# Second layer: row transfers held to their steps, norms of the finished batch moved into the expert stretch

## The reference, cut to what matters

```python
scores = jnp.einsum('bhqd,bhkd->bhqk', q, k) / sqrt(HD)
attn = jax.nn.softmax(scores, axis=-1)
ao = jnp.einsum('bhqk,bhkd->bhqd', attn, v)
x1 = _layernorm(x + ao @ Wo + bo, g1, be1)
...
topk_p, topk_i = jax.lax.top_k(gate_probs, K)          # K = 2 of E = 8
h = jax.nn.gelu(jnp.einsum('bsd,edf->bsef', x1, W1) + b1, approximate=False)
y = jnp.einsum('bsef,efd->bsed', h, W2) + b2
moe_out = jnp.einsum('bse,bsed->bsd', comb, y)
return _layernorm(x1 + moe_out, g2, be2)
...
x = x + _layernorm(_L0_ffn_ref(_layernorm(x, axis=-1), ...), axis=-1)
```

## Time and profile before

| what | value |
|---|---|
| median of 3 runs | 2871.48 us (2869.06 to 2873.38) |
| the profiled execution's own time | 2869.59 us |
| its span | 2867.9 us |
| busy: DVE, ACT, PE | 2243.4 us (78%), 1236.5 us (43%), 1195.6 us (42%) |
| POOL busy | 289.9 us (10%) |
| L1309, the maxima | 512 of 1219 ns |
| L1196, the exponentials | 512 of 1027 ns |

### The profile page before, as it was taken

How to read it: one execution, slowest core, us unless ns; L and a number is a source line. 1 busy time by engine, 2 the same in 40 slices (tenths; PEclk the granted TensorE clock), 3 DMA queues, 4 the chain that set the end, 5 groups by cost and what they waited for, 6 DMA issues and landing times. The chain is left out here.

```text
span 2867.9 us, 37860 instructions
## 1 busy us (share of the span) xinstructions
PE 1195.6 (42%) x7272; PEld 536.4 (19%) x7272; DVE 2243.4 (78%) x15187; ACT 1236.5 (43%) x3176; POOL 289.9 (10%) x425
## 2 busy tenths in 40 slices
PE   3010100101010000101004887788876887778697
PEld 1000000000000000000001111223421342133365
DVE  5999999999999999999975899856657665864133
ACT  1333333333333333333360556656655664567542
POOL 0000000000000000000010020031023212201211
PEclk9999999999999999999996899979987998889898
DMA  5000000000000000000034020103110212001100
GB/s 135 1 1 1 1 1 1 1 1 1 1 1 1 1 1 1 1 1 1 1 68 103 1 67 20 24 22 89 26 44 23 74 37 52 18 17 30 33 1 23
DMA packets 79603, 66.11 MB, mean 23 GB/s; under 512 B 8126, under 2 KB 64232, under 8 KB 79368
## 3 DMA queue, kind: packets, MB, share of 16 engines
q1 hardware_dynamic: 76296, 57.40, 8.3%
q0 software_dynamic: 3072, 6.30, 0.7%
HBM read 34.77 MB, written 28.57 MB: 22 GB/s over the span
## 5 line engine op out<-in xcount | busy, mean ns | idle before, releaser
L1309 DVE TENSOR_REDUCE nm_half<-pair 128x2 f32<-128x1024 f32 x512 | 611.7, 1219 | 224.1 <-PE pair L1557 188.6
L203 ACT ACTIVATE ex<-row,nmax 128x65 f32<-128x65 f32 x960 | 336.0, 350 | 923.8 <-DVE nmax L305 837.3
L1196 ACT ACTIVATE pt<-pair 128x1024 f32<-128x1024 f32 x512 | 510.2, 1027 | 389.2 <-PE pair L1567 357.9
L263 DVE SCALAR_TENSOR_TENSOR junk<-ex,tab 128x65 f32<-128x65 f32 x2850 | 620.0, 218 | 1.4 <-issue 0.4
L366 PE MATMUL p_s<-tab,bdg 128*128 128x32 f32 x120 | 31.9, 406 | 829.2 <-DVE tab L268 829.2
L1533 PE MATMUL p_o<-pt,va 128*9 128x512 f32 x2048 | 299.2, 659 | 9.7 <-ACT pt L1196 8.3
L268 DVE TENSOR_TENSOR tab<-raw,rz 128x1 f32<-128x1 f32 (+1 forms) x1890 | 284.8, 151 | 3.2 <-issue 1.1
L297 DVE SCALAR_TENSOR_TENSOR junk<-ex,rz,row 128x65 f32<-128x65 f32 x930 | 265.4, 285 | 3.0 <-issue 2.7
L1557 PE MATMUL pair<-ks,qs 48*128 48x512 bf16 x1024 | 212.8, 420 | 123.3 <-ACT pt L1196 75.4
L1567 PE MATMUL pair<-qs,ks 50*128 50x512 bf16 x1024 | 209.7, 414 | 62.4 <-DVE nm_half L1309 30.4
L263 DVE DVE_READ_ACCUMULATOR junk<-ex,tab 128x1 f32 x2850 | 233.8, 82 | 0.3
(11 more groups left out here) (254 smaller groups left out, 1908.1 us busy)
## 6 DMA issues: line engine op xcount, KB each, us to landing
parts_dram<-parts SPq DMA_DIRECT2D x48, 256.0 KB, 3.6
qs<-parts_dram SPq DMA_DIRECT2D x32, 192.0 KB, 4.8
ks<-parts_dram SPq DMA_DIRECT2D x32, 192.0 KB, 5.4
hid<-xs_dram SPq DMA_DIRECT2D x15, 256.0 KB, 2.9
ys_dram<-hid SPq DMA_DIRECT2D x15, 256.0 KB, 2.4
h_dram<-f SPq DMA_DIRECT2D x20, 128.0 KB, 2.5
x<-in_x SPq DMA_DIRECT2D x4, 512.0 KB, 8.4
w_W<-in_W SPq DMA_DIRECT2D x1, 2048.0 KB
```

Of the source, the lines that this page charges most:

```text
L203: nc.scalar.activation(ex[:, r % 2, :], row[:, r % 2, 1:], ACT.Exp, bias=nmax[:, r % 2:r % 2 + 1], accum_out=z[:, r % 2:r % 2 + 1]).then_i ...
L263: nc.vector.scalar_tensor_tensor(junk[:, g, :], ex[:, k, :], 1.0, tab[:, g, r:r + ROW], ALU.mult, ALU.mult, accum_out=raw[:, g:g + 1]).the ...
L1196: nc.scalar.activation(pt[:, kt % 2, :, tokens(t)], pair[fill.pair][:, :, :], ACT.Exp, scale=SCALE).then_inc(s_exp, 1)
L1309: nc.vector.reduce_max(nm_half[:, t, hp % 2, :, q], pair[fill.pair][:, :, :], AX.X, negate=True)\
```

## The change

It does four things. A step `SC` or `YG` carries a number, the count of exponentials that precede its step, and POOL waits for `s_exp` to reach it before it issues the step's two DMAs. The scatters are spread over steps 14 to 21 of the tables. The norms k=1 and k=2 of the finished batch move from steps 14 to 23 of `TAIL` to steps 27 to 47, and the two `ADD` move by a step. The phases start later and closer (29 to 54, every 5 steps), and the decays of `busy` and the floor of the maxima are changed. Between slots and the first scatter POOL also increments its pace semaphore once more.

```diff
--- before.py
+++ after.py
@@ -598,17 +598,18 @@
 
 AFTER = {0: [("AT", 0), ("AT", 1)], 1: [("WO", 0)], 2: [("LNS", 0, 0), ("WO", 1), ("LNS", 0, 1)],
          4: [("LND", 0)], 5: [("LNN", 0, 0)], 6: [("LNN", 0, 1), ("XT", 0)], 7: [("XT", 1), ("GL", 0), ("GL", 1)],
-         9: [("GA",), ("GE",)], 10: [("GB",)], 11: [("GC",)], 13: [("RK",)], 14: [("RT",)],
-         15: [("SC", 0), ("SC", 1)], 16: [("SC", 2), ("SC", 3)], 17: [("SC", 4), ("SC", 5), ("CT", 0)],
-         18: [("SC", 6), ("SC", 7), ("CT", 1)], 19: [("B2", 0), ("B2", 1)]}
-
-
-TAIL = {**{u: [("YG", u)] for u in range(QT)}, 8: [("XR",)], 12: [("ADD", 0)], 13: [("ADD", 1)], 14: [("LNS", 1, 0)],
-        15: [("LNS", 1, 1)], 16: [("LND", 1)], 17: [("LNN", 1, 0)], 18: [("LNN", 1, 1)], 19: [("LNS", 2, 0)],
-        20: [("LNS", 2, 1)], 21: [("LND", 2)], 22: [("LNN", 2, 0)], 23: [("LNN", 2, 1), ("OUT",)]}
-
-
-GROUP_AT = (26, 32, 38, 44, 50, 56)
+         9: [("GA",), ("GE",)], 10: [("GB",)], 11: [("GC",)], 13: [("RK",)],
+         14: [("RT",), ("SC", 0)], 15: [("SC", 1)], 16: [("SC", 2)],
+         17: [("SC", 3), ("CT", 0)], 18: [("SC", 4), ("CT", 1)], 19: [("SC", 5), ("B2", 0)], 20: [("SC", 6), ("B2", 1)],
+         21: [("SC", 7)]}
+
+
+TAIL = {**{u: [("YG", u)] for u in range(QT)}, 8: [("XR",)], 11: [("ADD", 0)], 14: [("ADD", 1)], 27: [("LNS", 1, 0)],
+        29: [("LNS", 1, 1)], 31: [("LND", 1)], 33: [("LNN", 1, 0)], 35: [("LNN", 1, 1)], 39: [("LNS", 2, 0)],
+        41: [("LNS", 2, 1)], 43: [("LND", 2)], 45: [("LNN", 2, 0)], 47: [("LNN", 2, 1), ("OUT",)]}
+
+
+GROUP_AT = (29, 34, 39, 44, 49, 54)
 
 
 FIRST_READY, READY = 1, 3
@@ -630,7 +631,9 @@
     if not attn:
         for steps in TAIL.values():
             for x in steps:
-                if x[0] in ("YG", "XR"):
+                if x[0] == "YG":
+                    yield "T", *x, 2 * QT * HP * s
+                elif x[0] == "XR":
                     yield "T", *x
         yield "PV", -1, QT - 1
         yield "OC", -1
@@ -687,7 +690,7 @@
     halves = in_turn(READY if moe else FIRST_READY, HP if last else HP + READY)
     total = len(halves)
     stream, waiting, due = [], [], []
-    busy = [0.0]
+    busy, scored = [0.0], [2 * QT * HP * s]
 
     def spent(x):
 
@@ -696,7 +699,7 @@
 
     def maxima(u, force=0):
 
-        least = 2 * u - 10 if moe else 5 * u // 2 + 1
+        least = 2 * u - 10 + max(0, u - 48) // 2 if moe else 5 * u // 2 + 1
         n = 0
         while halves and n < 1 + (not moe) and (n < force or total - len(halves) < least or busy[0] <= 0.9):
             x = halves.pop(0)
@@ -717,6 +720,8 @@
                     return
                 heavy = 1
             x = due.pop(0)
+            if name in ("SC", "YG"):
+                x = *x, scored[0]
             yield spent(x)
             if bank_uses(x):
                 return
@@ -727,7 +732,8 @@
         due += waiting
         waiting.clear()
         phase = moe and u in GROUP_AT
-        busy[0] = max(0.0, busy[0] - 1.9)
+        busy[0] = max(0.0, busy[0] - 1.7)
+        scored[0] = 2 * (QT * HP * s + u)
         yield "B", hp, kt, 0
         yield from maxima(u)
         if phase:
@@ -746,14 +752,14 @@
             yield from maxima(u, 1)
             while stream:
                 yield spent(stream.pop(0))
-            busy[0] = max(0.0, busy[0] - 5.0)
+            busy[0] = max(0.0, busy[0] - 3.0)
             stream += [("YS", j) for j in in_group(g)]
             due += [("XL", g + 2)] * (g + 2 < NG)
         else:
             for x in small():
                 passed.append(x)
                 yield x
-        busy[0] = max(0.0, busy[0] - 1.9)
+        busy[0] = max(0.0, busy[0] - 1.7)
         yield "B", hp, kt, 1
         yield from maxima(u)
         if u and not phase:
@@ -779,7 +785,7 @@
             due.append(("HR",))
         if moe:
             due += AFTER.get(u, [])
-            if u == GROUP_AT[0] - 6:
+            if u == GROUP_AT[0] - 7:
                 due += [("XL", 0), ("XL", 1)]
             if u + 5 in GROUP_AT:
                 due.insert(0, ("WC", GROUP_AT.index(u + 5)))
@@ -1138,6 +1144,8 @@
                                 pool.wait_ge(s_xs[i], group_loads(s - 1, NG - 2 + i))
                                 pool.sem_inc(s_pace_pool, 1)
                         pool.wait_ge(s_slots, s)
+                        pool.sem_inc(s_pace_pool, 1)
+                    pool.wait_ge(s_exp, x[2])
                     for k in range(2):
                         i = QT * k + q
                         nc.gpsimd.indirect_dma_start(
```

## The result

| | median | runs | ratio to before, 95% interval |
|---|---|---|---|
| before | 2872.39 us | 4 | |
| after | 2846.99 us (2842.57 to 2855.05) | 4 | 0.9917 [0.9895, 0.9939] |

The change saves 24 us by the ratio (25 by the medians); the forecast was 2852. The sum came out near, but three of its five terms did not. The profiled execution after took 2842.57 us (span 2840.8). The unchanged part up to the first exponential was 6.4 us shorter in it (1567.1 rather than 1573.5 us), so stages are compared, not ends.

What follows compares the result with a forecast made beforehand. DVE is busiest, but trains of 16 row transfers without a gap were taken to stall engines that all fall short of full. Terms -18-10+4+0+5 = -19 us gave 2852 us, range 2826 to 2876.

Steps and rivals of the forecast that it cites:

- YG: Gathers of batches 1 and 2 held over steps 2 to 9: gain 18 us of 27.5, one third put back.
- the tail: Last batch's gathers wait for exponential 512, 6.0 us later: +5 us, bounds 0 and +6.
- 24.9+25.8-2x11.6 = 27.5: Loss in us in steps 0 to 2 of batches 2 and 3 against batch 1, which the gather hold may save.
- SC: Scatters spread to step 22: half of 21 us in ACT gaps and half-clock matmuls saved, gain 10, bounds 0 and 21.
- Norms: Norms k=1 and 2 moved to steps 28 to 48: 18 us less in steps 12 to 25, 22 more later, +4.
- The 7.6 us: Excess of batch 2's steps 12 to 25 over batch 1's; less than half, 3 us a batch, taken as norms' least return.
- Paces: New decays and floor defer maxima, phases every 5 steps; counts equal: 0 us, bounds -4 and +6.
- A: Gaps behind pairs suffice, so gather and scatter holds give 27.5+21 us: 2832 us; chance 0.20.
- B: Spread transfers and DVE work get in each other's way, 14 us a batch, half on the path: 2866 us; chance 0.10.
- C: The stall belongs to each transfer, so spreading gathers and scatters saves nothing: 2880 us, slower; chance 0.14.
- D: Scatter waits do not bind because POOL is late by itself, scatter hold gives 0: 2862 us; chance 0.12.
- E: Moved norms' four square roots each stop ACT, another 4 us each, making +16: 2868 us; chance 0.08.

Runs made afterwards that it cites:

- e1: Kernel before with only the gathers (YG) held to steps, tail included: 2840.56 us, ratio 0.9903.
- e5: Kernel before with only the gather and scatter holds, phases one step later (27 to 57, every six): 2817.82 us, ratio 0.9817.
- e11: e5 plus the changed kernel's TAIL table, moving norms k=1 and 2: 2821.73 us, ratio 0.9843.
- e6: Changed kernel with the old decays (1.9 and 5.0) and old floor of the maxima: 2824.98 us, ratio 0.9829.
- e9: Kernel before with 14 of each batch's 16 gathers left out, sums using old data: 2832.83 us, ratio 0.987.
- e2: Changed kernel with scatters put back in their old places, without the wait for exponentials: 2878.85 us, ratio 1.0028.
- e3: Kernel before with only the new TAIL table, moving norms k=1 and 2: 2876.81 us, ratio 1.0024.
- e8: e1 with all 16 gathers held as one train until step 9 of the next batch: 2860.41 us, ratio 0.9953.
- e10: Changed kernel with the last batch's gathers not held in the tail: 2858.76 us, ratio 0.9961.

## Why the prediction came out right

The kernels make a path from before to after, each step one part: YG hold with the tail -30 (e1), SC hold with the phases one step later -23 (e5), norms +4 (e11), phases every five steps +3 (e6), decays and floor +22 (after). Together 2870.9 - 24 = 2847. The steps are differences of medians, each known to 6 to 10 us, so +4 and +3 can't be told from nothing and the others can.

1. *YG, and 5. the tail* (-18 and +5 forecast, -13 together): -30, of which the tail is -8 by the traces, so that some -22 is left for YG. The mechanism was right, and its size near. The row "24.9+25.8-2x11.6 = 27.5" was cut wrongly: the two stalls cost 10.4 us in steps 0 to 2 of batch 2 and 10.3 in step 63 before batch 3, and of the first the clock is a part (granted 0.61 there before, 0.89 after). The put-back was a fifth rather than a third (e9). For the tail the step "DVE goes on only when the train ends: +6" failed. Before, the free first 6 us of the train ran beside the last exponentials and the stall hit the chain behind them; now the chain itself runs beside the train (timeline after: first gather, and the output product's sum and the first norm under way while it runs):

```profile
2675.65 0.99 POOL L1182 DMA_INDIRECT yg<-ys_dram,slot_u  x1 [39.37 <-ACT pt L1205]
...
2681.27 0.69 DVE L1386 TENSOR_TENSOR xa<-p_o,hr 128x512 f32<-128x512 f32 x1 [2.64 <-PE p_o L1677]
...
2689.25 0.69 DVE L1409 TENSOR_TENSOR xa<-xa,w_g 128x512 f32<-128x512 f32 x1
...
2694.81 0.94 POOL L1182 DMA_INDIRECT yg<-ys_dram,slot_u  x1 [0.30 <-issue]
...
2698.28 0.19 DVE L1437 TENSOR_TENSOR logit<-p_o,w_bg 128x32 f32<-128x32 f32 x1 [5.13 <-remote]
```

In the earlier trace rows DVE did L1377 (now L1386) 16.7 us after the last exponential, here (last exponential done at 2675.38) 6 us after it.

2. *SC* (-10 forecast, at most -21): -32 taken from the changed kernel, -23 added to e1, where the late `XL` of batch 1 took 8 back. The mis-sized part is "half-clock matmuls behind, which I estimate at 3 a batch": 7.0 in batch 1 of e2. That the transfers' duty would leave half of the loss didn't hold either: at steps 19 to 22 after runs at clock 1.00.

3. *Norms* (+4): +6 alone, +4 with the holds. Right, also in its two halves: -18 and +22 forecast, -17.4 and +22.2 in the trace of e3, though 6.0 of what arrived lies in step 63 and not in steps 26 to 57. The 7.6 us from which the lower bound was taken is 10.3 by the exact starts.

4. *Paces* (0, -4 to +6): +39 alone, +22 to +25 with the holds. The step that failed is "Batch 0 runs on its floor of 5u/2+1 for most steps already". The counts were indeed nearly the same; what cost was in which half step the maxima lie, 12 us in batch 0, of which 4 are traced to a head pair's last one. "The counts are equal: 0" missed as well that what is put off must be paid at the batch's end, where nothing hides it.

The forecast was close because the two holds gave some 30 us more than it said and the paces took some 25 back: the way and the mechanism of the holds were understood, but that the sum came out within 5 us is luck. Of the rivals, A (stall vanishes) is nearest to what the holds do alone: they gave 53 where it had 27.5+21 = 48.5. Even so gaps of 2.9 us stand at the end of six transfers, so the stall did not vanish; the loss behind it had been priced too low. B: in the trace after scatters last 952/967/1273 ns (least, median, longest; in the earlier trace rows one took 2.16 us) and L1318 1221 ns as before, so nothing on the path is stretched by them (of 48 gathers three took 1.32 to 1.41 us, before the longest took 1.01); the exclusive lock that rival B goes by is not what limits here. The same section of the Trainium skill, "SBUF — State Buffer", "Who interferes with whom", says that PE and ACT never wait on anyone; what e8 shows, ACT idle 11.84 us beside a train, it does not explain. C, D and E fell with e1, e2 and e3.

Of what the prediction wanted to see, steps 0 to 2 of batch 2 (15.2) and its longer expert stretch (11.5 more) came as written; steps 0 to 2 of batch 3 took 18.7, behind the forced maxima; the pairs ran together; steps 12 to 25 came out at 50 to 56 rather than 60; and DVE did not wait 18 us after the last exponential.

What stays open: by which path the train stops the engines, and why so late. In e8 ACT stops 10.3 us after its start, DVE 11.4, and PE 13.9; in e10 ACT 11.8, in the tail before 6.0. No row names a releaser ("remote"). The DMA engines were only 18% busy in the gap of e8, so it is not that they were full; no run separates POOL's issuing from the data that moves, since e9 leaves out both.

## What to carry to other kernels

Look for places where every engine's wait ends "remote" at the end of a run of indexed transfers: let the run go out in pairs, held to the consumer's steps, and price such a stall with the half-clock stretch behind it, not with its gap alone. A combined change can hide a loss as large as its gain: here the two waits, with the scatters spread, are worth some 53 us and the rest took 29 back. When a planner's pace is changed, compare the place of each group's last element against its consumer, and what is forced at the end, not the counts.

## What the runs showed of the hardware

- A train of 16 indexed transfers (1.25 us apart) stops ACT for 11.84 and DVE for 11.49 us in e8, ACT for 9.59 in e10. ACT goes on 3.3 us after the last transfer was issued in e8 (2.6 in e10), DVE 4.0. Trains of eight cost 13 us over pairs in the whole kernel. Behind six transfers in the kernel after the gaps were 2.9 us.
- After the gap of 6 to 7 us in batch 1 of e2, PE was granted 1.2 GHz for some 16 us more, which cost 7.0 us.
- The granted clock over the first layer was 0.52 in nine of the profiled executions and 0.99 in five, and the lower did not make it longer: the first exponential of the second layer came at 1566.3 to 1570.8 us with the lower and at 1573.1 to 1574.4 with the higher. On the whole the runs of the kernel before differ little (on one chip a mean of 2869.8 us in 14 runs at a mean clock near 0.69, and 2870.8 in 9 near 0.94), those of e10 by 5 (2856.9 and 2861.7, six runs each).
